# The order of instructions and the turn of PSUM banks of a four-layer kernel, planned anew

## What is computed

```
x = L0(ctx, x)   # 16-head attention over [ctx; x] with queries from x, RMS norm, gelu MLP 256-1024-256
x = L1(x, ctx)   # RWKV-like layer: layer norm, token shift, five low-rank mixes, projections,
                 #   scan  s = a + w * s  over the 64 tokens in 32 heads of 8x8, group norm, gate,
                 #   then a channel mix  sigmoid(r) * (relu(k)^2 @ Wv)
x = L2(x, ctx)   # self attention, cross attention to ctx (masks multiplied in), gelu MLP
x = L3(x, ctx)   # cross attention, queries from x, keys and values from layer_norm(ctx)
```

## Time and profile before

| | |
|---|---|
| median of 3 runs | 1007.3 us (1005.73 to 1008.46) |
| the profiled execution's own time | 1010.23 us |
| its span, first to last instruction of the program | 1007.5 us |
| mean granted clock of TensorE | 0.986 |

### The profile page before, as it was taken

One profiled execution on the slowest core, in us unless ns is written; L12 is line 12 of the kernel. 1 busy time (PEld: TensorE's weight loads), 2 busy tenths in 40 slices (PEclk: granted clock), 3 DMA queues, 4 the chain that ended last, 5 costly groups with the idle time before them and its releaser, 6 DMA issues.

```text
span 1007.5 us, 27525 instructions
## 1 busy us (share of the span) xinstructions
PE 944.2 (94%) x10944; PEld 757.7 (75%) x10944; DVE 738.1 (73%) x1607; ACT 565.3 (56%) x1316; POOL 538.5 (53%) x662
## 2 busy tenths in 40 slices
PE   7979999997977999999999999999999999899997
PEld 4767887765756877878878788786767777788885
DVE  1685466889898888865755765777898798976665
ACT  2688642433333755677566678635744553586572
POOL 3464362565664457775246734564664665664341
PEclk9999999987989999999999999999999999999999
DMA  8004250000001001010111001100010000000001
GB/s 304 2 2 149 79 193 32 1 1 2 2 1 34 1 3 29 2 34 14 52 29 59 3 2 30 31 1 28 1 31 1 15 1 2 14 14 2 14 1 44
DMA packets 28589, 31.71 MB, mean 31 GB/s; under 512 B 14736, under 2 KB 25264, under 8 KB 27824
## 3 DMA queue, kind: packets, MB, share of 16 engines
q1 hardware_dynamic: 27440, 28.12, 8.7%
q10 hardware_dynamic: 1024, 1.85, 0.5%
HBM read 27.86 MB, written 2.10 MB: 30 GB/s over the span
## 4 chain that ended last, share of the span: by engine, by line
PE 62%; DVE 16%; DVEq 6%; issue 6%; POOL 4%; ACT 4%; POOLq 1%; DMA 1%; ACTq 0%; SPq 0%
PE bank L506 9%; PE bank L494 9%; PE bank L378 7%; PE bank L366 6%; PE bank L399 6%; PE bank L391 4%; PE bank L481 3%; PE bank L457 2%; DVE lane L1013 2%; PE bank L524 2%; PE bank L535 2%; PE bank L438 2%; DVEq L1016 2%; POOL lane L1423 2%; DVE bank L1009 1%
## 5 line engine op out<-in xcount | busy, mean ns | idle before, releaser
L1423 POOL TENSOR_TENSOR lane<-lane 128x512 f32<-128x512 f32 x160 | 165.8, 1043 | 164.8 <-DVE lane L887 88.8
L1189 ACT COPY lane<-bank 128x512 f32<-128x512 f32 x232 | 132.0, 591 | 129.8 <-PE bank L366 82.0
L366 PE MATMUL bank<-ident,lane 128*128 128x128 f32 x896 | 131.0, 278 | 8.8 <-POOL lane L1423 3.4
L366 PEld LDWEIGHTS bank<-ident,lane 128*128 128x128 f32 x896 | 102.8, 141 | 34.1 <-issue 10.5
L1495 POOL TENSOR_TENSOR lane<-lane 128x512 f32<-128x512 f32 x64 | 81.6, 1278 | 60.9 <-DVE lane L1013 60.4
L1171 ACT ACTIVATE lane<-bank,vecs 128x256 f32<-128x256 f32 x112 | 55.3, 549 | 55.6 <-PE bank L366 55.2
L1013 DVE TENSOR_TENSOR_SCAN lane<-lane,bank 128x256 f32<-128x256 f32 x128 | 80.9, 674 | 4.7
L885 DVE TENSOR_REDUCE lane<-lane 128x8 f32<-128x512 f32 x96 | 64.7, 674 | 17.1 <-ACT lane L1208 16.3
L1157 ACT ACTIVATE lane<-lane 128x256 f32<-128x256 f32 x96 | 52.4, 595 | 41.2 <-POOL lane L1408 41.0
L1485 POOL TENSOR_TENSOR lane<-lane 128x512 f32<-128x512 f32 x40 | 47.3, 1190 | 40.0 <-DVE lane L993 39.8
L1220 ACT ACTIVATE lane<-bank,vecs 128x256 f32<-128x256 f32 x128 | 51.7, 478 | 27.0 <-PE bank L494 26.6
(11 more groups left out here) (161 smaller groups left out, 2206.5 us busy)
## 6 DMA issues: line engine op xcount, KB each, us to landing
lane<-in_inT SPq DMA_DIRECT2D x16, 256.0 KB, 5.3
lane<-in_x SPq DMA_DIRECT2D x16, 256.0 KB, 3.1
w_d<-in_w_d SPq DMA_DIRECT2D x1, 3072.0 KB, 11.7
w_am<-in_w_am SPq DMA_DIRECT2D x1, 2048.0 KB, 10.1
lane<-in_inT SPq DMA_DIRECT2D x16, 128.0 KB, 3.1
lane<-in_ctx SPq DMA_DIRECT2D x8, 256.0 KB, 2.8
out_x<-lane SPq DMA_DIRECT2D x8, 256.0 KB, 2.2
w_c<-in_w_c SPq DMA_DIRECT2D x1, 1792.0 KB, 7.9
```

Of the source, the lines that this page charges most:

```text
L366: ins = pe.transpose(t[:, i * P:(i + 1) * P], src, ident[:, :])
L1189: s.copy(out, src).then_inc(bk.free_sem(key), 1)
L1423: p.tensor_tensor(q, q, den.unsqueeze(2).to_broadcast([P, n, 512 // n]), ALU.mult).then_inc(sig["normal"].sem, 1)
```

## The change

Only the five strings of `ORDER` and the string `BANKS` are replaced. Every engine has the same pieces, with the same instructions, in the same order within a lane. The interleaving differs locally: 342 of 865 places of TensorE's stream hold the piece they held before, 374 of 785 on VectorE, 289 of 673 on ScalarE, 199 of 473 on GpSimd and 32 of 60 on SyncE; a piece is moved by about one place in the mean (1.15, 0.94, 1.10, 1.18 and 1.03), on TensorE by 21 at most. Here are the pieces at the places that the text speaks of, counted out from the strings.

The diff, without most of `BANKS`:

```diff
--- before.py
+++ after.py
@@ -81,56 +81,56 @@
 
 ORDER = {
     "PE": (
-        "P3330000101011121022022012313002012210201100011301020113123030012023103003000102002331112101321103310313200200"
-        "03000012011223230003222133013301022221102101121011131033300211320103200102222122013022022000300312203312300133"
-        "01133332103002332310010013123320100300003000000012300020302213311201222012013130310232032101002012303203322320"
-        "31133301112012123003111121010121111120221020123001112022222222222012202221302020010300102000200122213233202202"
-        "12023020031002120030021210112210023203233310303023332303231031232110311020310122232122221212320231001321302012"
-        "31122222122221210011111113022233313033012301202301131231121113033211023322301131323232031213133312310330333331"
-        "00302110130223131133131330323330301002003232322100013113103212321310001132123332222003233310231222122221312320"
-        "13313032233213123131311222113111311133132313120130133323333333333121333223131210012010323033333"
+        "P3303000010111102012222012133002012201201100101301020311132101320302003300002000013232111013112031301312300002"
+        "03000020112213230003323213202010322120211102111011012133003331112030200102122221230200220020000312321323030313"
+        "30111333300233023012001103231201300030000300000021030020302231311210202212001313103320320010122201303023322323"
+        "01313311120121233010011111200211122112102011201113021222222022202202320222102020000031002102000222132312202132"
+        "02032002030020201002123101122110022303333102303023333203132021332110311031020112222132202212222301301321302012"
+        "31122222120222111211110113022233331300312301201231031231121110332311232230311130322323031213133213310333033303"
+        "10032011130223131113331330233330300202013300132220010311313021232113001132123332220203233310231222212211220323"
+        "21323312303313113131312121112113231133231031312131333333333333312313320313221121002313023330303"
     ),
     "DVE": (
-        "P0300001102011100112002112232210220012200010011001113110331013303322323122212231330323302330300320320032300000"
-        "01100001010101100122011111102111123200310020002000020102023202022003310221312203100300000033033332100003330323"
-        "02110321211311133111012031002001030202112020222122221331223032303233301331313112310113121203211001330031100212"
-        "21222022022322000220001200233002133333333020201111132212222112230203212020023202203221301222000210002122022202"
-        "20012002110113001123121021111110133133331322310013211002002020020200222222001130223212332301331033211203310232"
-        "31113233113331332031113231023010300001001021212202021233220013202323201313113111113333331112133233122311321322"
-        "11223322222130212123211211021112331331333313133333131030013330020333333333332331331322322121011210213312121333"
-        "133230032330133"
+        "P0301000001001201111202112213220220012200010011011103110331031302132312222331333223003232330300032032032300000"
+        "01100001001101100212011111102111102023100300202000200100222002322000132131322320103000000033330330012033330023"
+        "02110231211311133110123101002010003210201220221221122323203232303330123331133112131310122310210011333100120102"
+        "21322202202220220200002100232133030333333020230111122121222122003221312200302020222203221300212000022211202200"
+        "02210022110113002111132012111110113333331122330102131002200020020200202222210013222321332301331033211203310332"
+        "21113233113133233133110213200310300100010201212020222133200213022303121233113111113333331121133331222311312322"
+        "11223322222132021213212110112133112133133133333333131300333010200333333333333132331302231112211212311322013333"
+        "133223301320303"
     ),
     "ACT": (
-        "P3303001010101200121202011231120220202012001001101103113013313023202232001033123233110201133023302000300223231"
-        "32213310111100110202002002320212030200020030003031133100313000201010113000000102130231100020302011321200123200"
-        "32120310223221130302023333013123201111203011203030311021211112220020220001001221102222233210222031320120010221"
-        "11232232203022310212020203022202330121112222233322301123121110201333110210113222231130331031320231021311202202"
-        "22110000131303031323330131131112300233032332332323232013033330000212100211323212310131330303121300120012112112"
-        "32112101233222323223103132311021012322232131333033010313323111113233333212332111301320231302333021311221133323"
-        "1120330333333"
+        "P3303000101101002001221211211320220022012001010101103113301133202312003020233321230310211133023300020300223223"
+        "31313201111010211200020001023220023202000000303013313310103000021010131000000101230121030020200331121200001232"
+        "32211031032222013032203303133231211011302112003331010201211112220220200010012112321222230033202220121200002112"
+        "22231312230021221032020200222002331312122122233332012211231110013233110310211122202311303313320231021311200222"
+        "00122100131330301323313031311112003233322330332323231320033330000122100211323213102131333031231000020111221113"
+        "22111210233222323223131032311210102223223113333303103133301111123233332321332100113132131333323121213133202031"
+        "1232303333033"
     ),
     "POOL": (
-        "P0121002330101102212002010113103302322130023330001002302010300100001111001221111101011312230020200022002222033"
-        "02012132230030303003331003333100002121113311120123032200212221231323033031131321112011302301221122022123020020"
-        "22233333301031221122300202000232033320012100020200202110011211201313032213002021220200222221001232223311031131"
-        "02231101313132321111030030002121200232321032310033113031121333313132331221221323122212213131212123231313333311"
-        "331313303333033333201230211213333"
+        "P0301002010121231212020010113130320312312300233000002300300021010001111001221111100111122003320200200022202203"
+        "31133000302320302233031003333010011221013311121020303022212121232323033031133121112011332003122112210222200232"
+        "23203033030311222213001220000220302033201300122000021210011211210031322331002120220200202222211220323131301131"
+        "32201103113123311110030020320121002233221021303003311323131313311233331212221321322221213131121223311233333311"
+        "331103333033333330331122121023333"
     ),
     "SP": (
-        "3032120131200132P0P1P23P000000112022222311131213333302132013"
+        "3023003012131221PPP0123P000000122012222331111213333302131203"
     ),
 }
 BANKS = (
-    "01234567024351672035104653101740617420165716354762321605326104307542370675601456012424537243647306524074063104"
...
+    "01234567023415670234102531460572305172304536014567037261072364061576104205243752437656250614501265403216302173"
...
```

More of the change, by code:

```diff
@@ L123 @@
 BANKS = (
-    "01234567024351672035104653101740617420165716354762321605326104307542370675601456012424537243647306524074063104"
-    "57630514620314265314053214065312543015627317453672450372504530745302147357042317541237516324750474176451730251"
-    "46700302517302461573025671535167351067263527136356327413056675643560132461075342536241560327154032671546017531"
-    "27543127605431542157315643125764031321405214037537635276713527346516521065712651726173052645156723145602724357"
-    "24351724635105305031507312546701324675064173250673425137046137061372501372564013725640163147647316047231504654"
-    "71605427362103205610365247147316741063751023750162473625342607534256031765043127506431725072065742064205367214"
-    "50235160742351075347035217043604530642531041205420637542176053024201452073154627627351627437054317054361326127"
-    "06706375012635714035712605473601602615042162516204657134657613674501637504167357307534015737263727623476037463"
-    "14067351324051324601732460173246024176024135604721435165041376520437652043170643572031256704312564037512640234"
-    "673546517302651372"
+    "01234567023415670234102531460572305172304536014567037261072364061576104205243752437656250614501265403216302173"
+    "65230176540376547610753610745315603714625031546024137042137043270541372502145307247253045730261240654106726354"
+    "01225724637256017432507231714752470512432740572247051236720723765123064132075647564173542613724153076401276457"
+    "36503712465037501572017340521736403456324056324104710571760574031567460246730743607431260260275406327546162162"
+    "31762130576243515073165073264501732450614753612054360753241756075641327645017362451703621467145627041623752675"
+    "06743516052171024571240565651365213576243104621370564702564071256401253160742315670351426742760432763270654713"
+    "26015246735201673205367021536453765430657267423650174623514063752715673251467026052176054124372643172072057265"
+    "46546063720546327416327410536217217420751241024710523047602304376250347625034764762465702464316434136513715631"
```

(2 more changed lines are left out.)

## The result

The changed kernel takes 990.26 us (median of 4 runs, 989.68 to 992.27), the kernel before beside it 1007.88 (4 runs): ratio 0.9825, interval 0.9807 to 0.9844, 17.6 us faster. A later comparison on another occasion gave 991.34 against 1010.19, ratio 0.9817 (0.9799 to 0.9835). The forecast was 999.3: the sign was right, the gain was more than twice the 8.0 us of the sum.

The account below looks back on a forecast made before the run. TensorE, busy 944.2 of 1007.5 us, was taken as the bound, with VectorE the limit in the scan stage. Terms 3.0 + 3.0 + 2.0 + 0.7 + 1.0 + 1.3 - 3.0 = 8.0 us off 1007.3 gave 999.3; range 988 to 1010.

Parts of the forecast that it names:

- Near 200 us: Scan stage: three held-back pieces of group 3's MLP fill TensorE's gap ahead of 1:sum0; 3.0 us won, upper end 3.87.
- Near 245 us: Scan stage: three projections of group 0 ahead of group 3's lora fill TensorE but delay lane 3; 2.0 us won.
- Near 295 us: Scan stage: TensorE loses 6.6 us, but VectorE's 0.73 us of idle time is the limit; 0.7 us won.
- Near 757 us: scores ahead of rstdr fills TensorE's wait for rsqrt, and rsqrt moves two places forward; 3.0 us won.
- Table loads: Six ScalarE loads fewer, 37 left; only the pair in 50 to 100 us shows, by half, 1.3 us won.
- The end: Last 32.5 us: group 7's pT0 ahead of two projections, and a 1.91 us gap inside 6:wt1; 1.0 us won.
- What the shuffle gives back: About 500 changed places of TensorE's stream may get inputs late; three gaps, 3.0 us lost.
- Banks and SyncE: Bank turns right only for their order, an unread bank costs a wait; SyncE's moves costed at nothing.
- most of it is reached: Rival: TensorE's whole loss near 200 and 757 us goes, upper ends elsewhere, nothing given back; 18.4 us, 988.9; chance 0.15.
- The clock doesn't follow the order: Rival: gaps close but others of the same cost open, so no clock gain; 3.7 us, 1003.6; chance 0.10.
- T: Theory tested in the experiments: the time came from TensorE's gaps and the slow clock behind them.
- Slower: Rival: at 245 us group 3's lora waits behind three projections, 5.7 us, and lane 3 ends last; 1013; chance 0.12.

Follow-up runs that it names:

- b_757: Kernel before with only the two local moves near 757 us (scores ahead of rstdr, rsqrt ahead of tot0 and mask3): 1008.56 us, ratio 0.9997.
- s_second: Order and banks of the kernel before up to about 460 us, of the changed kernel from there: 1003.47 us, ratio 0.9949 to the kernel before.
- a_757: Changed kernel with TensorE's order near 757 us put back (h1, h2, rstdr, scores): 992.16 us, ratio 0.9857 to the kernel before.
- s_first: Order and banks of the changed kernel up to about 360 us, of the kernel before from there: 1006.14 us, ratio 0.9971 to the kernel before.
- b_psum2: Kernel before with rsqrt's scratch t in the PSUM bank instead of SBUF, bank given back after the last step: 1013.46 us, ratio 1.0048.
- b_clock: Kernel before with overwritten matmuls ahead of seven TensorE waits, only to keep the engine busy: 1004.23 us, ratio 0.9964.
- a_757dve: Changed kernel with VectorE's order near 757 us put back (rsqrt behind tot0 and mask3): 998.67 us, ratio 0.9898 to the kernel before.

## Why the forecast was right in sign and wrong in size

The step that failed is the way the sum was made: I looked for the places where TensorE had lost time and put VectorE's loss at those places as the limit. In the scan stage VectorE is the engine to follow, and its loss had to be added up over the whole stage: 24.1 us of idle time and 5.9 us of holds in round 1, of which the forecast counted 7.6 and 0.9. "VectorE's work there can't be shortened by more" was said of the windows and taken for the stage. What the order then took away was mostly the holds, 12.8 us of 15.6 in the whole kernel, of which the sum had priced three steps. Two smaller terms failed beside it: the table loads (1.3 for 4.7) and the 3.0 charged for the shuffle.

- *Near 200 us*, 3.0: the lead grew by 4.7 from 177 to 218 us, and the gap is closed as described. But b_757 and s_second, which have the old order there and no slow clock, gain 3.1 of these 4.7 us as well. So 3.1 us, the slow clock among it, were bad luck of the one execution that I read, and 1.6 are left for the order. The medians don't rest on it: the profiled executions are 19.5 us apart, the medians 17.6.
- *Near 245 us*, 2.0: it grew by 4.4 from 218 to 263 us, and by 2.8 in the changed kernel's second profile; the upper end was 3.9. I had halved it for the delay handed to lane 3, which didn't come: group 3's last scan step ends at 297.7 us for 310.7. The windows also have two holds, of 0.51 and 0.84 us, where I had counted one of 0.93.
- *Near 295 us*, 0.7: 0.9 from 263 to 343 us, of the right size, but in another way: 1.9 us lost at the new hole near 280 us, 2.8 won behind it.
- *Near 757 us*, 3.0: 3.7 by the lead from 737 to 776, and 2.7 more up to 846. Close in size, but the reason was half of it: undoing TensorE's part (a_757) costs 1.2 us by the trace, undoing VectorE's part 6.1. I had also read two holds of 0.93 us out of windows that have one; the three there are of 0.31, 0.38 and 0.93. I had costed rsqrt's move as a delay of tot0 and mask3 and had not seen that the delay is what keeps GpSimd off it.
- *Table loads*, 1.3: undoing them costs 4.7 us by the median (5.8 by the ratios) and 3.9 by the trace. "TensorE is full and hides them" was wrong for the pair near 495 us (1.68 us of wait) and right for the third. A load also has no drain behind it in the new rows (495.05 and 1.28, then the gelu at 496.35), and so it is for 34 of the 37 loads (the gelu or Exp starts 0.01 us behind): here the trace stands against the 2.66 us for a switch that the forecast gave from the Trainium skill (ScalarE: Activation LUTs, What ACT_TABLE_LOAD costs).
- *The end*, 1.0: the gap of 1.91 us is still 1.84, and the lead fell from 21.7 to 18.2 between 846 and 979 us, 1.3 coming back behind that.
- *What the shuffle gives back*, -3.0: from 384 to 703 us, where hundreds of places changed, the lead went from 14.1 to 14.4. What the new order does give back is the 1.9 us at the hole near 280 us and the 3.5 of the last 140 us, and both are counted at their places here. Beside them nothing of the 3.0 is seen, and that is an error about as large as the one of the table loads.
- *Banks and SyncE*, 0: the banks of the new order cost nothing, as taken; s_first, b_757 and b_psum2 show what they cost when they don't fit, 1 to 5 us each.

Of the signs named: the wait on L1051 is gone, the loads are 37, 450 to 600 us is unchanged in what TensorE does, and TensorE's waits of over 1 us are 14 for 17 (from 25 us on). The clock was to be 0.95 or more from 200 to 300 us and is 0.97 and 0.90: wrong, and it mattered little. The window of 200 to 325 us was to be shorter by 4 us; from 218 to 343 us it is 5.3.

Of the rivals, *most of it is reached* (988.9) came nearest by its time, but by its mechanism it is T at its upper ends, with most of the holds left out; that its sum comes near is luck. *The clock doesn't follow the order* is partly true: b_clock puts the clock's share at 3.6 to 4.1 us, while 13.6 of the 27.2 us of low clock are still there in the changed kernel. *Slower* fell: what lora of group 3 waited didn't reach the end of the stage, which is 11.4 us shorter.

The parts as measured by themselves: holds about 6.1 us, table loads 4.7, the clock 4.1, together 14.9 of 17.6 (by the ratios 5.0, 5.8 and 3.6, together 14.4). Each is uncertain by 2 to 3 us, they were measured in different kernels and may overlap, and of the holds only an equal amount of other work was measured. So the order of size is shown and the shares are not; what is left, some 3 us, stays open. So does the loss of 3.5 us between 846 and 979 us, which no experiment took apart.

## What to carry to other kernels

Where several in-order engines share a stage, take the engine with the least free time and add up its whole loss over the stage, holds by other engines among it, before looking at TensorE's gaps; filling a gap of 5.7 us brought nothing here, and one VectorE piece moved by two places cost 6 us. Compare each instruction's longest and median duration: a sum of excesses over the median is a budget that a mere order can win, here with about half of it showing in the time. Look also at where the slow clock falls: inside VectorE's stage it cost between nothing and 1.5 us, and just behind its end 2 to 3 us. And profile the kernel before more than once, or a slow stretch of one execution is taken for a thing to win. An order is only as good as its banks: move a piece, and look first who still reads the bank that it will get.

## What the runs showed of the hardware

The same instructions in the same order get a different clock from one execution to the next. Up to that point a_757 and the changed kernel don't differ; at 55 us their windows are, the changed kernel first:

```profile
55.00:60.00 5.00, 3.57 (x84) 3.03 (x84) 4.71 (x13) 5.00 (x17) 3.29 (x4) 1.00 0.00 0
```

```profile
55.00:60.00 5.00, 2.90 (x84) 2.38 (x74) 4.22 (x11) 4.97 (x18) 3.29 (x5) 0.77 0.00 0
```

Such a stretch cost about 2 us here (the lead of a_757 at 142 us is -1.3 for 0.7), and the one unedited kernel run twice differs by 1.5 us between 211 and 251 us for this reason alone. The Trainium skill (TensorE: Matmul & The Clock Gate, What's actually happening) says that the gate runs freely and not in step with the kernel; this trace agrees, and one profile's lead can be read to about 2 to 4 us only. It may be why a_757dve is 8.4 us slower by the median of four but 6.1 at its place; that was not shown.

GpSimd's hold makes a 0.23 us instruction of VectorE last until 0.08 us behind the end of the GpSimd operation beside it, 0.83 to 1.15 us, three in a row in a_757dve. It took instructions with two SBUF inputs (L962, L981, L1045, L1047, L1049, L1078), and also L949 and L1042 with one, SBUF to SBUF (L949 1255 ns at most for a median of 348 in the changed kernel); L1047 with an input in PSUM was never held.
